# A modulated four-layer convolution on one core: its opening with the first pair's cross copies on ScalarE and VectorE

## What is computed

```python
def _layer(x, style, w, b, mw, mb, typ):
    s = style @ mw.T + mb
    weight = SCALE * w * s[:, None, :, None]
    demod = lax.rsqrt(jnp.sum(weight * weight, axis=(2, 3)) + EPS)
    weight = weight * demod[:, :, None, None]
    if typ == 'same':         out = jax.vmap(_conv_same)(x, weight) + b[None, :, None]
    elif typ == 'upsample':   out = _blur(conv_up(x, weight) + b, 2.0 * blur_k, (1, 1))
    elif typ == 'downsample': out = conv_down(_blur(x, blur_k, (2, 2)), weight) + b
    return out

out = x
for i, typ in enumerate(('same', 'upsample', 'same', 'downsample')):
    out = _layer(out, style, weights[i], biases[i], mod_w[i], mod_b[i], typ)
return x + out
```

## Time and profile before

| | us |
|---|---|
| median of 3 runs | 656.19 |
| lowest, highest run | 655.96, 658.18 |
| the profiled execution's own time | 656.46 |
| its span, first to last instruction | 654.7 |
| PE busy in the span | 642.8 (98%) |
| DVE, POOL, ACT busy | 541.8, 396.5, 383.5 |

### The profile page before, as it was taken

One profiled execution on the slowest core, in us unless ns is written; L12 is line 12 of the kernel. 1 busy time (PEld: TensorE's weight loads), 2 busy tenths in 40 slices (PEclk: granted clock), 3 DMA queues, 4 the chain that ended last, 5 costly groups with the idle time before them and its releaser, 6 DMA issues.

```text
span 654.7 us, 13058 instructions
## 1 busy us (share of the span) xinstructions
PE 642.8 (98%) x4771; PEld 616.6 (94%) x4771; DVE 541.8 (83%) x680; ACT 383.5 (59%) x738; POOL 396.5 (61%) x361
## 2 busy tenths in 40 slices
PE   8998999999999999999999999999999999999997
PEld 7797999999999999999999999999999999999986
DVE  5989977989898787889998987777989997777872
ACT  4456457666556665655766655666555666665541
POOL 3357667655567655467765666755657766566630
PEclk9999999999999999999999999999999999999999
DMA  7258868689777878886789878778977778988783
GB/s 261 52 120 205 198 168 205 175 220 221 183 182 186 211 202 221 202 188 156 201 200 224 196 179 219 175 198 207 232 153 206 177 192 214 230 202 196 189 207 122
DMA packets 146991, 125.64 MB, mean 192 GB/s; under 512 B 6064, under 2 KB 113648, under 8 KB 146928
## 3 DMA queue, kind: packets, MB, share of 16 engines
q1 hardware_dynamic: 146560, 124.56, 76.4%
q10 hardware_dynamic: 368, 0.25, 0.2%
HBM read 36.51 MB, written 33.75 MB: 107 GB/s over the span
## 4 chain that ended last, share of the span: by engine, by line
PE 91%; DVE 4%; issue 1%; POOL 1%; ACT 1%; DMA 1%; SPq 0%; DVEq 0%; ACTq 0%; POOLq 0%
PE po L202 13%; PE po L203 13%; PE po L204 13%; PE pg L202 8%; PE pg L204 8%; PE pg L203 8%; PE pm L204 5%; PE pm L202 5%; PE pm L203 5%; PE pg L207 4%; PE pg L208 4%; PE po L454 1%; DMA V<-Vx 1%; PE pe L445 1%; PE pg L454 1%
## 5 line engine op out<-in xcount | busy, mean ns | idle before, releaser
L202 PE MATMUL po<-xh,W 128*128 128x256 f32 (+1 forms) x640 | 199.7, 312 | 2.0 <-issue 2.0
L203 PE MATMUL po<-xl,W 128*128 128x256 f32 (+1 forms) x640 | 199.5, 312 | 0.0
L204 PE MATMUL po<-xh,W 128*128 128x256 f32 (+1 forms) x640 | 198.8, 311 | 0.0
L202 PEld LDWEIGHTS po<-xh,W 128*128 128x128 f32 x640 | 125.2, 196 | 7.2 <-issue 2.2
L204 PEld LDWEIGHTS po<-xh,W 128*128 128x128 f32 x640 | 125.5, 196 | 5.8
L203 PEld LDWEIGHTS po<-xl,W 128*128 128x128 f32 x640 | 126.0, 197 | 5.0
L820 DVE TENSOR_TENSOR xl<-X,xh 128x1290 fp32r<-128x1290 f32 x64 | 127.7, 1996 | 1.8 <-ACT xh L556 0.8
L617 ACT CAST Gh<-Gf 128x512 fp32r<-128x512 f32 x64 | 39.7, 622 | 124.7 <-DVE Gf L851 124.7
L556 ACT CAST xh<-X 128x1290 fp32r<-128x1290 f32 x64 | 88.1, 1376 | 20.8 <-PE po L204 15.1
L829 DVE SCALAR_TENSOR_TENSOR T<-po,DD,M 128x512 f32<-128x512 f32 x96 | 71.3, 743 | 33.3 <-ACT M L563 21.3
L563 ACT ACTIVATE M<-pm,cv,DD 128x256 f32<-128x256 f32 x96 | 54.2, 564 | 71.7 <-PE pm L204 71.5
(11 more groups left out here) (175 smaller groups left out, 1743.1 us busy)
## 6 DMA issues: line engine op xcount, KB each, us to landing
X<-in_xin SPq DMA_DIRECT2D x64, 516.0 KB, 4.4
out<-T SPq DMA_DIRECT2D x64, 512.0 KB, 6.0
W<-W SPq DMA_DIRECT2D x93, 256.0 KB, 4.3
W<-W SPq DMA_DIRECT2D x31, 384.0 KB, 5.6
V<-V SPq DMA_DIRECT2D x32, 256.0 KB, 5.0
V<-W SPq DMA_DIRECT2D x32, 128.0 KB, 4.4
V<-Vx SPq DMA_DIRECT2D x32, 128.0 KB, 4.1
E<-in_ed SPq DMA_DIRECT2D x1, 768.0 KB, 7.2
```

Source lines behind the costliest of these rows:

```text
L202: eng.matmul(o, wh_, rh, start=first, stop=False)
L203: eng.matmul(o, wh_, rl, start=False, stop=False)
L204: return eng.matmul(o, wl_, rh, start=False, stop=last)
```

## The change

The change touches the opening and the first two groups. The cross halves of samples 0 and 1 are made by five copies on ACT and three on DVE (two functions `cross_first`), and SP keeps only those of samples 2 and 3. conv(0) waits for these copies and for a high and low part of the first 516 columns of X only, which are made ahead of the rest, before POOL's subtraction. Newton's three steps are separate calls with other work between them. The two products `constant` move from the units of the prologue to behind conv(0), the product with E to behind the prologue, and `final` to a place inside sample 0's work. Cl, A2l and Q3f change engines (A2l from DVE to POOL, Q3f of groups 1 and 2 from POOL to ACT), input transfers change order, warm-up counts change (3, 5 and 22 become 5, 4 and 14), and two POOL waits are added in `x_parts(1)`.

```diff
-WARM3 = 22
+WARM2, WARM3 = 4, 14
@@ sync
                                 ("bb", ...),
-                                ("a2", A2f[:], a2),
                                 ("b1", ...),
                                 ("mwt", MW[:, 0:2], mw[:, 0:2]),
+                                ("a2", A2f[:], a2),
...
-            cross_pair(0)
-            cross_pair(1)
+            cross_second()
@@ tensor, conv(b)
-                    pe.wait_ge(s_w[g % 2], 2 * 16 * ND * (g // 2 + 1))
+                    if g == 0:
+                        pe.wait_ge(s_wxh, 3)
+                        pe.wait_ge(s_wxl, 2)
+                        pe.wait_ge(s_x0h, 1)
+                        pe.wait_ge(s_x0l, 1)
+                    else:
+                        pe.wait_ge(s_w[g % 2], 2 * 16 * ND * ((g + 1) // 2))
...
-                if q == 0:
+                if q == 0 and n or b == 1:
@@ tensor, the list
             scales(P3).then_inc(s_pp, 1)
-            warm(3, pg[3])
+            pe.wait_ge(s_in["b1"], 16)
+            pe.wait_ge(s_ek, 3)
+            static_sums(0, last=False)
+            pe.wait_ge(s_in["mwt"], 16)
+            pe.wait_ge(s_sc, SC_S)
+            scales(0)
+            scales(1).then_inc(s_pp, 1)
             pe.wait_ge(s_sq, 1)
             pe.wait_ge(s_sc, SC_SQ2)
             energy(2).then_inc(s_pp, 1)
...
+            warm(5, pg[3])
             pe.wait_ge(s_a2, 1)
             for x in PROLOGUE[:2]:
                 unit(*x)
...
-            for t in range(3):
-                m = pe.matmul(pe_[0:64, 0:128], E[0:64, 1, t, 0:64], ...)
-            m.then_inc(s_pp, 1)
-            warm(5, po[1])
+            warm(WARM2, po[1])
...
             for x in PROLOGUE[4:7]:
                 unit(*x)
-            constant(2, 1, SC_K2)
             for x in PROLOGUE[7:]:
                 unit(*x)
-            constant(3, 3, SC_K3)
+            for t in range(3):
+                m = pe.matmul(pe_[0:64, 0:128], E[0:64, 1, t, 0:64], ...)
+            m.then_inc(s_pp, 1)
             warm(WARM3, po[1])
             conv(0)
+            constant(2, 1, SC_K2)
             for b in range(B):
                 for x in units_of(b):
                     unit(*x)
...
+                if b == 0:
+                    constant(3, 3, SC_K3)
@@ scalar
+            def cross_first(u, v):
+                act.copy(W[hi, 0, u, 0, 0, 1], Wf[lo, 0, u])
+                act.copy(W[lo, 0, v.start + 1:v.stop + 1, 0, 0, 1], Wf[hi, 0, v]).then_inc(s_wxh, 1)
...
-            x_high(0)
+            act.wait_ge(s_x[0], 16)
+            act.copy(xh[:, 0, 0:2 * HW], X[:, 0, 0:2 * HW]).then_inc(s_x0h, 1)
+            q3_full(1)
+            q3_high(1)
             high(0, 2)
             high(0, 3)
             act.wait_ge(s_sc, SC_D)
             identity(0)
-            q3_high(1)
             high(0, 4)
+            cross_first(slice(0, 2), slice(0, 2))
+            x_high(0)
             high(0, 6)
+            cross_first(slice(2, 5), slice(2, 4))
+            act.wait_ge(s_wl, 2)
+            act.copy(W[lo, 0, 3:5, 1, 0, 1], r32(W[hi, 0, 2:4, 1, 0, 0])).then_inc(s_wxh, 1)
             sums_high(0)
@@ gpsimd
+            pool.tensor_tensor(A2l[:], A2f[:], r32(A2h[:]), ALU.subtract).then_inc(s_a2, 1)
             pool.tensor_tensor(Cl[:], Cf[:], r32(Ch[:]), ALU.subtract).then_inc(s_cl, 1)
+            q3_low(1)
+            pool.wait_ge(s_x0l, 1)
             x_parts(0)
-            pool.wait_ge(s_sc, SC_D)
-            q3_full(1)
-            q3_low(1)
-            q3_full(2)
+            x_parts(1)
             q3_low(2)
-            pool.wait_ge(s_wl, 2)
-            x_parts(1)
@@ vector
+            def cross_first(u, part):
+                dve.wait_ge(s_wl, part + 1)
+                m = dve.tensor_copy(W[hi, 0, u, 1, 0, 1], r32(W[lo, 0, u, 1, 0, 0]))
+                if part == 0:
+                    m = dve.tensor_copy(W[lo, 0, 1:3, 1, 0, 1], r32(W[hi, 0, 0:2, 1, 0, 0]))
+                m.then_inc(s_wxl, 1)
...
             dve.wait_ge(s_sc, SC_A)
             dve.wait_ge(s_ss, 3)
+            link(newton(slice(0, 3), t01, 0))
+            q2_low(0)
+            link(newton(slice(0, 3), t01, 1))
             dve.wait_ge(s_k0, K_B1D)
             tt(B1dl[:], ...).then_inc(s_b1d, 1)
-            link(newton(slice(0, 3), tmp[:, 0:3]))
+            link(newton(slice(0, 3), t01, 2))
...
             for b in range(B):
                 g, i = divmod(b, NG)
-                if b == 4:
-                    edges_begin()
...
                 if b == 0:
                     g_low(1)
+                    final()
...
                     x_low(2 * g + 1)
+                if b == 4:
+                    edges_begin()
```

More of the change, by code:

```diff
@@ L464, in energy, with static_sums @@
                 return m
-            def static_sums(d):
+            def static_sums(d, first=True, last=True):
                 p = lo if d else slice(0, 128)
@@ L470, in static_sums, with add @@
                 x = b1t[p]
-                def add(c, i, n, rhs, first, last=False):
-                    return pe.matmul(pb[d][:, i:i + n], EK[c][p, at], rhs, start=first, stop=last)
+                def add(c, i, n, rhs, start, stop=False):
+                    return pe.matmul(pb[d][:, i:i + n], EK[c][p, at], rhs, start=start, stop=stop)
                 end = x[:, 2:3].to_broadcast([64, 2, C]) if d else x[:, 2:3]
@@ L477, in static_sums @@
                 n = 2 if d else 1
[L478 to L486, removed]
+                if first:
+                    add(0, 0, 2, x[:, 0:3:2], True)
+                    add(2, 2, 2, x[:, 0:3:2], False)
+                    add(0, 4, n, end, False)
+                    add(0, 3, 1, x[:, 0:1], False)
+                if last:
+                    add(2, 1, 2, x[:, 0:3:2], False)
+                    add(1, 1, 2, x[:, 1:4:2], False)
+                    add(3, 2, 2, x[:, 1:4:2], False)
+                    add(1, 3, 1, x[:, 1:2], False)
+                    return add(1, 4, n, end3, False, True)
             pe.wait_ge(s_dm, 1)
@@ L497, in _ @@
             energy(2).then_inc(s_pp, 1)
[L498 to L506, removed]
+            static_sums(0, first=False).then_inc(s_bp, 1)
+            pe.wait_ge(s_ss, 1)
+            for n, l in enumerate((0, 1, 3)):
+                pe.wait_ge(s_sq, n + 2)
                 m = energy(l)
             m.then_inc(s_pp, 1)
+            warm(5, pg[3])
             pe.wait_ge(s_a2, 1)
@@ L646, in _ @@
             act.copy(B1h[:, 0:5, 1, :], pb[0]).then_inc(s_k0, 1)
+            act.wait_ge(s_in["cw"], 16)
+            act.copy(Ch[:], Cf[:]).then_inc(s_k0, 1)
             act.wait_ge(s_sc, SC_A)
@@ L1015, in _ @@
             g_low(0)
+            reached(tt(inv3[:], AA[:, P3], DD[:, P3], ALU.mult))
+            dve.wait_ge(s_x0h, 1)
+            tt(xl[:, 0, 0:2 * HW], X[:, 0, 0:2 * HW], r32(xh[:, 0, 0:2 * HW]), ALU.subtract).then_inc(s_x0l, 1)
+            full(0, 4)
+            reached(dve.tensor_scalar(tmp[:, 0], DD[:, 1], bias(0), None, ALU.mult))
             dve.tensor_scalar(tmp[:, 1], S[:, P2], bias(1), 2.0, ALU.mult, ALU.mult)
+            w_low(0, 0)
+            full(0, 5)
+            full(0, 6)
+            cross_first(slice(0, 2), 0)
             dve.wait_ge(s_pp, 5)
@@ L1019, in _ @@
             reached(tt(tmp[lo, 1], tmp[lo, 1], kt[lo], ALU.add))
-            full(0, 4)
-            full(0, 5)
-            full(0, 6)
-            w_low(0, 0)
+            w_low(0, 1)
+            cross_first(slice(2, 5), 1)
+            sums(0)
+            full(1, 0)
+            full(1, 1)
+            sums_low(0)
+            q2_low(1)
+            x_low(0)
             dve.wait_ge(s_pp, 6)
```

115 lines of the change are left out of this document (55 added, 60 removed).

## The result

Seven runs of the changed kernel gave a median of 653.63 us (653.2 to 654.51), seven of the kernel before beside them 658.14 (655.93 to 659.14): a ratio of 0.9941, interval 0.9923 to 0.9960. The median of before hangs on few runs. In the later comparisons it was 656.26 (29 runs), 656.27 (28), 656.36 (20) and 657.08 (11); against these the change is worth 0.4 to 0.5%. The forecast of 653.4 and its range, 652.1 to 655.4, hold, and the size is at the edge of what a measurement of this kernel tells.

What follows compares the result with a forecast made beforehand. PE, busy without a break from 100 us, was taken as the bound, so the gain lay in the waits before: 2.2 at conv(1) plus 0.54 at unit (2,5), 2.75 off 656.46; median forecast 653.4 us, range 652.1 to 655.4.

Steps and rivals of the forecast that it cites:

- The root: Opening up to unit (0,2): new order worth 0, kept at -0.2 to +0.5; unit (0,2) at 16.7 for 17.04.
- The block at G: DVE's low parts of G meet POOL's low parts of Q3: ends at 22.5, unit (0,4) at 21.8, unblocked 21.3.
- The filter's low part: Group 0's filter on DVE: second low part ends at 29.45 for 28.69 before, 0.75 late.
- The copies: First pair's cross halves copied instead of transferred: 0.4 for the last copy replaces 3.8 us, data for conv(0) at 29.9.
- the rival of dear copies: Copies ahead of conv(0) slower than before's transfers: conv(0) at 36.9, time 660.4; slower by over 0.5% given 0.04.
- The warm-ups: PE ahead of conv(0): 14 warm-ups at 0.24 end at 29.9, with the data; conv(0) 3.95 earlier.
- Given back: Between conv(0) and conv(1): two constants' products at 0.87 each cost 1.74, leaving conv(1) 2.2 earlier.
- That this wait would not shrink: At conv(4): group 1's low parts and cross transfers move by 2.2 with conv(1), so the wait of 2.05 stays.
- The end: From conv(4) to the last matmul: the wait of 0.54 at unit (2,5) goes, so 0.54 is gained.
- PE is busy for every microsecond from 100 us on: Unbroken PE stretch from 100 us: nothing on other engines shortens it; the opening's value is when it begins.
- The quicker opening: DVE before POOL at G (0.5), group 1's low parts without POOL (0.9): gain 2.75 to 4.1, down to 652.1; chance 0.36.

Runs made afterwards that it cites:

- ten-warm-up run: Changed kernel with 10 warm-up matmuls instead of 14 ahead of conv(0): 654.89 us, ratio 0.9977.
- short constants: Changed kernel with one matmul instead of three in each of the two constants' products: 652.06 us, ratio 0.9930.
- the hold: Changed kernel with one more POOL wait: group 3's low parts of Q3 start only after group 1's low parts of W: 654.47 us, ratio 0.9959.
- copies alone: Kernel before with only the first pair's cross halves made by ACT and DVE copies, 18 warm-ups for 22: 657.91 us, ratio 1.0023.
- pairs with the block ahead and the hold: Changed kernel, groups 1 to 3's cross transfers issued by sample pairs, DVE's edge operations ahead of conv(4)'s eviction work, POOL's Q3 low parts held: 654.26 us, ratio 0.9957.
- pairs alone: Changed kernel with the cross transfers of groups 1 to 3 issued by pairs of samples: 652.75 us, ratio 0.9930.
- pairs with hold: Changed kernel, groups 1 to 3's cross transfers issued by sample pairs, POOL's Q3 low parts held, edge operations left in place: 652.32 us, ratio 0.9927.
- block in the gap: Changed kernel, cross transfers by sample pairs, POOL's Q3 low parts held, edge operations in DVE's idle gap ahead of the sample's low part: 651.4 us, ratio 0.9905.

## Why the prediction held, step by step

**The root** was taken at 0; the first Newton chain and group 0's Q3f start within 0.1 of before (8.93 for 8.84, 10.27 for 10.22). Unit (0,2) starts at 16.85 for the forecast 16.7 (17.04 before): the last low part ahead of it took 0.42 as forecast, but the pair of them starts 0.23 later, behind the second Newton chain's first step.

**The block at G** was priced in full, at 0.55, and cost 0.21. DVE's first low part of G began at 20.60 for 20.4, while POOL's second part of Q3 ran until 20.94, so that they met for 0.34; it took 0.89 there and 0.68 where POOL was idle (37.93). By the Trainium skill's page "SBUF — State Buffer", section "Who interferes with whom", the two shut each other out for the whole instruction; this trace agrees but for 0.13 to 0.14 us: the DVE instruction that met POOL here, and the two that met it in the earlier trace rows, ended 0.55, 0.28 and 0.08 behind POOL's, and alone they take 0.68, 0.42 and 0.22. Unit (0,4) came at 21.64 for 21.8.

**The filter's low part** ended at 28.82 for 29.45. POOL's two subtractions of the first sample, put at 1.6, took 0.64 and 0.70, and the first low part of W ended at 25.31 for 25.65. **The copies** were priced at 0.3 on the way and 0.4 at the end, and took 0.29 and 0.42; the row of 1.14 was a wait, as taken, and the rival of dear copies falls.

**The warm-ups**: the data were there at 29.3 and not at 29.9, but the fourteen warm-ups held PE, so conv(0) came at 29.76 for 29.9. The ten-warm-up run, in which conv(0) starts 0.37 behind the last copy, shows that only 0.1 was lost by them.

**Given back**: this term was too small. From conv(0) to conv(1) PE took 7.56 before and takes 9.54 now, 1.98 more, for 1.74: each constant's product costs about 1.0 with the first matmuls around it, not the 0.87 of its row. Since conv(0) gained 4.09 for 3.95, the two misses nearly cancel, and 2.11 is left for 2.2. There is no wait at unit (1,2), and `final` is covered. conv(1) at 39.30 for 39.2, conv(4) at 56.86 for 56.8, behind a wait of 2.02 for "about 2". That this wait would not shrink was the step that kept the gain at 2.2 while conv(0) gained 4.1.

**The end**: between conv(4)'s start and the last matmul the kernel before took 591.26 and the changed one 590.57, a difference of 0.69 for 0.54. At unit (2,5) 0.76 is gained, the wait of 0.54 and what PE lost in restarting behind it; at conv(8) 0.32 is lost in the same way, with the new wait of 0.16, which the prediction did not have. Of the 0.23 that remain, 0.19 come near the end, where PE waits for the last V, whose transfer took, before and now:

```profile
636.25 5.24 DMA V<-Vx
```

```profile
633.60 5.07 DMA V<-Vx
```

So the prediction's sentence that PE is busy for every microsecond from 100 us on reaches further than its row, which ends at 200: in the last group both kernels wait some 2 us in all. The times of this stretch also differ between profiles. DVE's low part in it took 2.67 with the changed kernel, and 1.76 with the short constants, where PE came from 619 to the last V 0.8 faster:

```profile
624.58 2.67 DVE xl L848
```

```profile
624.28 1.76 DVE xl L847
```

The sum was 2.75 and 2.82 came. That they agree to 0.07 is in part luck: the products, conv(8) and the last transfer were missed, with both signs. Before's profile, moreover, lies 0.5 above its runs at the full clock and the changed kernel's 0.1, so that by these runs the gain is 2.4.

**The quicker opening**, the first rival, did not come: its first half, no block at G, came for the most part (0.21 was left of it), but the filter's data then waited for the warm-ups; its second, group 1's low parts without POOL, did not happen: 2.51, for 2.48 in the earlier trace rows. The short constants and the hold show that this half can come and what it is worth at conv(4): 0.5 to 0.6.

What the prediction lacked is the clock: it treated the profile at 1.000 as the kernel, though 54 of 88 later runs of before lay under 0.998. That moved the median of before by 1.9 us between two comparisons, two thirds of the gain forecast.

## What to carry to other kernels

A wait that the change leaves standing can be worth as much as the one it removes: conv(0) gained 4.1 us, of which 2.1 reached conv(4), while splitting the transfers at that next wait by their first reader gave 0.9 more and, with POOL held back and the work that the wait had covered moved into an idle gap on its engine, 2.2. Before a wait is taken away, list what other engines do during it; here it was DVE's edge block, and with POOL held back the same block was worth 2.35 us of waiting in one place, 0.88 in another and none in the third. A few small copies on engines that have just produced the data beat transfers of the same halves, 0.46 against 3.8 us from the low part's end until the halves are there, but only if the engine's other work for the same reader is moved out of the way first.

## What the runs showed of the hardware

The granted clock of PE fell from 2.4 to 1.2 GHz for some 3 us behind a wait of about 2 us at conv(4) in some executions, and in others, of the same kernel and behind the same wait, not. Two other waits of PE were followed by such a fall in a profile: that of 1.75 for the constant (copies alone) and that of 2.35 at unit (2,5) (pairs with the block ahead and the hold). The 18 runs of the three kernels whose profiles show no wait over 1.1 us between 30 and 80 us (pairs alone, pairs with hold, block in the gap) all stayed at 0.998 or more. With a longer wait the share of runs below varies, and not by the wait's length alone: 54 of 88 of before and one of seven of the changed kernel, both with some 2.0 at conv(4), seven of twelve with 1.45, one of six with 1.50. What sets the lowest level of before, 0.993 to 0.994 at 659, no profile at hand shows; the only profile with two falls, that of the copies alone, has 0.995.

The same DVE subtraction pair took 1.68 us without POOL's Q3 beside it and 2.51 with it, and the 64x128 copy 0.22 and 1.14; where the two only met for 0.34, at G, it cost 0.21. A SBUF-to-SBUF transfer of 128 KB landed 3.1 us behind its issue, and 256 KB in a queue of four 6.6, while the copies that replace such transfers, of 64 and 96 KB each, took 0.3 to 0.5 on DVE or ACT.
